# Weighted sums of four attention steps in one block, with four probability buffers and a later load of the gathered rows

## The reference

```
xn  = layernorm(x) * g1 + b1
q,k,v = split(xn @ w_in.T + b_in)            # 16 heads of 16
scores = q @ k.T / 4                          # masked: row i sees all columns if i % 8 == 0, else only itself
x1  = x + (softmax(scores) @ v) @ w_out.T + b_out
h   = x1 + gelu((layernorm(x1) * g2 + b2) @ w1.T + c1) @ w2.T + c2
y   = layernorm(x + h)
out = layernorm(y + F(y))                     # F: relu(y @ wi.T + lora_e) @ wo.T, e = argmax of 8 gate logits per row
```

## Time and profile before

| | us |
|---|---|
| median of 3 runs | 1441.14 |
| lowest and highest | 1438.82, 1443.34 |
| span of the profiled execution | 1437.3 |
| TensorE busy | 1386.3 |
| VectorE busy | 854.4 |
| ScalarE busy | 734.6 |
| GpSimd busy | 647.8 |

### The profile page before, as it was taken

How to read it: one execution, slowest core, us unless ns; L and a number is a source line. 1 busy time by engine, 2 the same in 40 slices (tenths; PEclk the granted TensorE clock), 3 DMA queues, 4 the chain that set the end, 5 groups by cost and what they waited for, 6 DMA issues and landing times.

```text
span 1437.3 us, 26412 instructions
## 1 busy us (share of the span) xinstructions
PE 1386.3 (96%) x10103; PEld 1066.3 (74%) x10103; DVE 854.4 (59%) x1823; ACT 734.6 (51%) x1103; POOL 647.8 (45%) x533
## 2 busy tenths in 40 slices
PE   6799999999999999999999999999999999999997
PEld 5688665678888766668888866667888876556996
DVE  6748576636656666555647576763675657762332
ACT  3444555553544555564444555555444455655442
POOL 3554321328754414145865432333776442132755
PEclk9899999999999999999999999999999999999999
DMA  7565223215561132212682213220556212310100
GB/s 246 161 181 107 57 45 67 55 38 192 190 164 47 50 68 51 56 45 84 210 214 62 74 38 75 57 53 20 189 189 158 74 45 44 80 26 23 52 16 30
DMA packets 91394, 130.51 MB, mean 91 GB/s; under 512 B 8314, under 2 KB 68180, under 8 KB 88148
## 3 DMA queue, kind: packets, MB, share of 16 engines
q1 hardware_dynamic: 91268, 128.82, 32.9%
HBM read 68.08 MB, written 60.57 MB: 90 GB/s over the span
## 4 chain that ended last, share of the span: by engine, by line
PE 79%; DVE 10%; POOL 4%; issue 2%; ACT 2%; DMA 0%; SPq 0%; POOLq 0%; DVEq 0%; ACTq 0%
PE ps L1567 19%; PE ps L1568 16%; PE ps L1569 16%; PE ps L1756 8%; PE ps L1745 7%; PE ps L1730 4%; DVE mx L1442 3%; PE ps L1803 2%; PE ps L1791 2%; PE ps L1825 2%; DVE stats L1316 2%; POOL rows L1042 1%; ACT prob L1172 1%; PE ps L1688 1%; PE ps L1762 1%
## 5 line engine op out<-in xcount | busy, mean ns | idle before, releaser
L1442 DVE TENSOR_REDUCE mx<-ps 128x2 f32<-128x1024 f32 x256 | 311.1, 1223 | 179.0 <-PE ps L1730 176.9
L1172 ACT ACTIVATE prob<-ps 128x1024 f32<-128x1024 f32 x256 | 262.6, 1026 | 180.4 <-PE ps L1745 180.2
L1057 POOL TENSOR_TENSOR hid1l<-gel,hid1h 128x512 fp32r<-128x512 f32 x85 | 111.2, 1309 | 202.2 <-ACT hid1h L1214 202.1
L1057 POOL TENSOR_TENSOR hid2l<-gel,hid2h 128x512 fp32r<-128x512 f32 x85 | 111.1, 1307 | 197.6 <-ACT hid2h L1214 197.5
L1057 POOL TENSOR_TENSOR hid0l<-gel,hid0h 128x512 fp32r<-128x512 f32 x86 | 112.4, 1307 | 191.6 <-ACT hid0h L1214 191.5
L1206 ACT ACTIVATE gel<-ps,cols 128x512 f32<-128x512 f32 x128 | 88.2, 689 | 180.7 <-PE ps L1569 169.5
L1745 PEld LDWEIGHTS ps<-qslot,kslot 50*128 50x128 f32 x1024 | 76.2, 184 | 91.0 <-issue 65.8
L1208 ACT ACTIVATE gel<-ps 128x512 f32<-128x512 f32 x128 | 76.6, 598 | 120.9 <-PE ps L1825 119.7
L1756 PE MATMUL ps<-prob,vals 128*32 128x256 f32 x2048 | 137.5, 385 | 0.2
L1745 PE MATMUL ps<-qslot,kslot 50*128 50x256 f32 x1024 | 128.9, 330 | 4.2 <-ACT prob L1172 4.1
L1730 PE MATMUL ps<-kslot,qslot 48*128 48x512 f32 x512 | 105.8, 424 | 4.8 <-DVE mx L1442 4.4
(11 more groups left out here) (245 smaller groups left out, 3943.9 us busy)
## 6 DMA issues: line engine op xcount, KB each, us to landing
k_d<-kst SPq DMA_DIRECT2D x192, 128.0 KB
kslot<-k_d SPq DMA_DIRECT2D x64, 384.0 KB
xin<-in_L_attn_x SPq DMA_DIRECT2D x32, 256.0 KB, 4.3
rows<-xs_d SPq DMA_DIRECT2D x16, 512.0 KB, 6.3
y_d<-rows SPq DMA_DIRECT2D x15, 512.0 KB, 3.1
rows<-y_d SPq DMA_DIRECT2D x15, 512.0 KB, 4.5
out<-rows SPq DMA_DIRECT2D x15, 512.0 KB, 3.2
xs_d<-xin SPq DMA_DIRECT2D x28, 256.0 KB, 2.7
```

Source lines behind the costliest of these rows:

```text
L1057: nc.gpsimd.tensor_tensor(hid[i % RING][1][:], gel[i % 2][:], hid[i % RING][0][:], ALU.subtract).then_inc(lo_done, 1)
L1172: nc.scalar.activation(prob[(n - 1) % 2][:].rearrange("p e i q -> p (e i q)"), ps[:, 0:2, :].rearrange("p a n -> p (a n)"), ACT.Exp).then_ ...
L1442: nc.vector.tensor_reduce(best[:, :, j % NQ], ps[:, at:at + 2, :], AX.X, ALU.max).then_inc(maxr_done, 1)
```

## The change

The probabilities get four buffers. The third lies over `xg` and the end of `x1g`, the fourth over `x1o`. The weighted sums of steps s-4 to s-1 are put ahead of every fourth step; near the end two stand ahead of step 62 and two behind step 63. The gathered rows are loaded at step 63, not 4, because their place now holds probabilities.

```diff
+GROUP = 4
@@ moves
-            if s == 4:
+            if s == STEPS_B - 1:
                 put(("ldg", b))
@@ step
-            if s % 2 == 0:
-                weighted(s - 2)
-                weighted(s - 1)
+            if s and s % GROUP == 0:
+                for one in range(s - GROUP, s):
+                    weighted(one)
+            elif s == STEPS_B - 2:
+                for one in range(s - 2, s):
+                    weighted(one)
@@
+def prob_of(p, kk):
+    s = p * KK + kk
+    return (s + 2 * (s >= STEPS_B - GROUP)) % GROUP
+
+PROB_FREE, _user = {}, {}
+for _s in STEPS:
+    if _s[0] == "sc":
+        _k = prob_of(*_s[2:])
+        PROB_FREE[_s[1:]] = _user.get(_k, 0)
+        _user[_k] = COUNT[_s]
@@ placement
-        prob = [place(f"prob{i}", [P, 2, 2, QW], F32, m0 + 4096 * i)[0] for i in range(2)]
+        prob = [place(f"prob{i}", [P, 2, 2, QW], F32, at)[0] for i, at in enumerate((m0, m0 + 4096, r1 + 3072, r1 + 8192))]
@@ SP, ldg
-                    sp.wait_ge(stq, 48 * KT * N("pq", b))
+                    sp.wait_ge(av_done, N("at", b, PAIRS - 1, KK - 3))
                     sp.dma_start(xg[:], x_v[b, :, :, 0, :]).then_inc(xgld, 16)
@@ GpSimd, xc
+                    if b and PLACE[c] < 3:
+                        pool.wait_ge(av_done, N("at", b - 1, PAIRS - 1, KK - 3))
@@ ScalarE, sc
-                    else:
-                        act.wait_ge(av_done, n - 2)
-                    nc.scalar.activation(prob[(n - 1) % 2][:].rearrange("p e i q -> p (e i q)"),
+                    elif a[1:] == (0, 2):
+                        act.wait_ge(stq, 48 * KT * N("pq", b))
+                    elif a[1:] == (0, 3):
+                        for k in range(2):
+                            act.wait_ge(x1st[k], max(v for (bb, _), (j, v) in X1_STORE.items() if j == k and bb == b))
+                        act.wait_ge(xs_done, N("stx", b, CHUNKS[-1]))
+                    if a[1:] > (0, 3):
+                        act.wait_ge(av_done, PROB_FREE[a])
+                    nc.scalar.activation(prob[prob_of(*a[1:])][:].rearrange("p e i q -> p (e i q)"),
@@ TensorE, at
-                            last = mm(ps[at:at + PR, OUT, 0:QW], vals[:, v:v + PR], prob[(n - 1) % 2][:, e, i, :],
+                            last = mm(ps[at:at + PR, OUT, 0:QW], vals[:, v:v + PR], prob[prob_of(p, kk)][:, e, i, :],
```

## The result

The changed kernel takes 1451.82 us (median of 6 runs, 1450.14 to 1454.11) where the kernel before, on the same chip, takes 1441.62 (6 runs, 1438.82 to 1444.48). The ratio is 1.0081, 95% interval 1.0066 to 1.0095: slower by 10 us, where I forecast no difference (1440.4) and a range of 1432 to 1448.

What follows compares the result with a forecast made beforehand. The prediction took TensorE's in-order queue as the bound (79% of the chain, busy 96%). Its terms, -8.4 + 12.6 - 4.9 = -0.7 us, taken to the median 1441.14, gave 1440.4 us; 8-in-10 range 1432 to 1448.

Steps and rivals of the forecast that it cites:

- Fewer blocks: TensorE, attention phases: merging weighted sums saves 0.14 us of block edges, 15 times in 4 batches, -8.4 us.
- What a block covered, VectorE: Steps losing their block: maxima wait for VectorE's reduce, 3.0 us in each of batches 0 and 3, 2.0 in others.
- What a block covered, ScalarE: Steps losing their block: scores wait for the exponential, 0.7 us per batch in 0 and 3, 0.6 in others.
- What the longer block covers: Steps 4, 8, ..., 60: the block grows by 0.86 us, VectorE catches up and maxima wait less, -4.9 us.
- The collision rule: VectorE with two SBUF inputs and GpSimd block each other; collisions could disappear or come, some 3.6 us either side.
- Four buffers, new waits: Exponentials wait for the sum that last used their buffer, steps 2 and 3 for stores: none late, 0.
- Gathered rows late: Load at step 63 delays GpSimd's next hidden tile to 658.2 from 656.1, covered by idle time: cost 0.
- B: Rival: VectorE becomes the bound within three steps without block, at maxima of steps 3, 7, 11, ...: 1453 us, chance 0.12.
- A: Rival: VectorE's jobs slip into the gaps without holding the maxima: 1430.4 us, half of it 1435.5; chance 0.27 with halves.
- C: Rival: the late load holds GpSimd so that TensorE waits, 2 us in each of 4 batches: 1448 us, chance 0.04.
- D: Rival: the merged block takes the same time per wave as two blocks, edges stay: 1448.8 us, chance 0.04.

Runs made afterwards that it cites:

- outer_only: The changed kernel with groups of four in batches 0 and 3 alone, blocks of two steps in batches 1 and 2: 1449.48 us against 1440.53 before.
- half kernels: The kernel before and the changed kernel, each with VectorE's maximum reduce over 256 of 512 columns: 1426.69 and 1420.86 us.
- best: Changed kernel with own blocks at steps 6, 10, 42 (batches 0, 3) and 14, 50 (1, 2), gate's jobs held in 0 and 3: 1433.83 us.

## Why the prediction was wrong

The profiled span came out 12.0 us above the one that I had summed. The terms in us over the four phases are worked out from the starts on TensorE: each step's interval from scores to scores after, less that before, where a block taken out counts as -1.00 and one that grew as +0.86. The maxima's row is the change from scores to maxima, the next two from maxima to what follows them. Batches 0 and 3 are taken from outer_only's batch 3, which had the full clock, twice.

| term | forecast | measured |
|---|---|---|
| blocks | -8.4 | -8.4 |
| maxima waiting, less relieved (forecast 10.0 less 4.9, measured 13.6 less 5.2) | +5.1 | +8.4 |
| the matmul behind waiting maxima | 0 | +1.6 |
| the small transpose behind relieved maxima | 0 | +2.1 |
| exponential (measured 2.5) and rest | +2.6 | +3.2 |
| stretches at half clock | 0 | +2.9 |
| outside the phases | 0 | +1.5 |

- *Fewer blocks*: right. 1.86 for a block of 32 and 0.14 saved a block. The drain that the Trainium skill gives in TensorE: Matmul & The Clock Gate, Single matmul latency, would have made 10.5 of it, as an estimate; the trace's own row was right.
- *What a block covered, VectorE*: this is the step that failed, in its price. The mechanism was right, and at the places that I had named so was the lateness of the maxima, but for one. The maxima of steps 11 and 43 wait 0.62 more each (forecast 0.6), those of 23 and 27 0.86 and 0.99 more (forecast 0.9), of step 50 in batch 1 0.96 (forecast 0.95). I took each of these as if nothing came of it elsewhere. Step 14 of batches 1 and 2 waits 1.41 and not 0.55, 1.7 us in all, by the new collision. Seven steps of batches 0 and 3 that I had put at nothing (6, 7, 19, 22, 30, 31, 51) wait 0.05 to 0.28 more, 1.5 in all. And the matmul behind waiting maxima comes 0.1 us late too, as the half kernels show: 2.6 us by its own starts, of which 1.0 in batches 0 and 3 is not lost, since the next scores wait for the exponential anyway. This was in the trace of before (the maxima of step 9 start at 179.63, 0.43 behind the scores, in the earlier trace rows; the matmul after them starts another 0.43 later), yet I never read that second interval. Together my waits and relief were to come to +7.7 us net; they came to +15.3 at full clock.
- *What a block covered, ScalarE*: right, 2.5 us where I had 2.6.
- *What the longer block covers*: failed in batches 0 and 3. Of "0.60, 0.5 go" the maxima gave back all of it, and the transpose behind them took it: 0.54 more at step 13 and at 45, 1.05 to 1.1 a phase. I had looked at the waiter that the row names, not at who waits next. In batches 1 and 2 the 1.44 did go from these maxima (0.84, 0.38 and 0.20), but the first of them came back at step 14.
- The collision rule: I had given it 3.6 us to either side. Its new collision came, at step 14 of batches 1 and 2 (0.45 to 1.31), and no collision in batches 0 and 3 went away by itself. best avoids one in batches 0 and 3 by holding the gate's jobs, and keeps the one at step 13 of batches 1 and 2 (1.30 in batch 1), with a block of its own ahead of step 14 to cover it. The Trainium skill's SBUF — State Buffer, Who interferes with whom, calls it an exclusive lock, which VectorE's operations with two SBUF inputs and GpSimd's that read SBUF contend for; the trace agrees, 1.25 beside 0.19 for one operation.
- The clock: I took the 1.00 of the earlier trace rows as given and put what a wait does to the clock at nothing, without a reason; it came to 2.9 us. The granted clock of the runs of the changed kernel is 0.989 to 0.992, of the kernel before 0.992 to 0.996.
- *Four buffers, new waits* and *Gathered rows late*: right, each 0, shown each by a run.
- The rivals: B is nearest to what came, by its sign and its threshold. It asks for more than 0.30 us lost per removed block: by the table 8.4 + 1.6 + 2.1 + 3.2 and the 5.2 of relief that maxima showed, over 60, is 0.34, without the clock. Its place came only in batches 0 and 3 (steps 11, 23, 27 and 43, which I had in the forecast itself); batches 1 and 2 have no new wait at steps 3, 7, 11. Its price, 1453, is close to 1451.82 partly by luck, as 2.9 us of clock and 1.5 outside the phases were no part of it. I gave it 0.12 because I asked whether the losses could double at VectorE, and not what each one drags behind it. A, C and D did not come.

What stays open: why some stretches at half clock come and others don't. The changed kernel's fell behind waits at steps 6 and 23, but one at 83 us, in a projection phase that all kernels share, came in half of the kernels, and of the three versions that keep blocks chosen alone had one in a phase (batch 3, step 3). There is one profile of each kernel, so that the waits bring these stretches is argued from where they lie and from the lower granted clock of the runs, not shown by an experiment of its own. Some 0.7 us of the table's exponential and rest lies in intervals that I did not assign to a cause.

## What to carry to other kernels

A block of matmuls that others wait on is also the time in which the slower engines catch up. Before it is merged with another, list for each gap what they do in it, and price a new wait by three things: the lateness itself, the next instruction behind it, and what an engine that is brought forward then meets (another waiter, or another engine's operation). A relief is priced in the same way. Merge only where the slower engine has idle time of at least the block's length, and put its loose jobs into the long blocks that result: here this turned a loss of 10 us into a gain of 6.7 (4.3 of it in the phases).

## What the runs showed of the hardware

- In this kernel a TensorE matmul that has waited for a semaphore delays the one behind it: 0.43 us from start to start, not 0.33, and about 0.40 where the wait itself is too short to be seen in a start.
- Two VectorE operations with two inputs lasted until GpSimd's beside them ended: 1.31 us, not 0.45, and 1.25, not 0.19. An edit that only shifts VectorE by 0.84 us made the first of these.
- Short waits can come with a loss of clock. Behind the wait of 1.34 us at step 23 the clock was granted at half for 3.4 us, and the block in it took 2.94 us, not 1.86. Such a stretch cost 1.3 to 1.7 us. Waits of 1.28 and 1.42 us elsewhere in the same run had none behind them.
- The idle time that a page names for a releaser can be far below what it costs: 4.4 us were named for the maxima of the kernel before, their starts were 10.6 us late, and with the short reduce the kernel gained 12.5.
